# A two-layer convolution kernel on one Trainium2 core: an earlier sine table, an earlier second x load, and another order of ScalarE's and GpSimd's first steps

## What is computed

```python
def _implicit_filter(z, w1, b1, w2, b2, w3, b3, wo, freq, t, deltas):
    h = jnp.sin(freq * (z @ w1 + b1))
    h = jnp.sin(freq * (h @ w2 + b2))
    h = jnp.sin(freq * (h @ w3 + b3))
    h = h @ wo
    decay = jnp.exp(-t * jnp.abs(deltas))
    return h * decay
...
k = jnp.einsum('ijk,imk->ijmk', hx, hy)[0]
...
out = y + x * bias[:, None, None]
...
scores = jnp.einsum('bpsd,bptd->bpst', x, x) * inv_dim
red = jnp.sum(scores * weights[None], axis=-1, keepdims=True)
y = x + red
y_hat = (y - mean) * jax.lax.rsqrt(var + BN_EPS)   
return y_hat * gamma[None, :, None, None] + beta[None, :, None, None]
```

## Time and profile before

| | |
|---|---|
| median of three runs | 969.54 us |
| the profiled execution | 969.15 us |
| its span (first to last instruction) | 967.2 us |
| TensorE busy | 942.9 us, 97% |
| VectorE, ScalarE, GpSimd busy | 749.7, 684.9, 672.1 us |
| TensorE's mean granted clock | 0.993 of full speed |
| read and written in DRAM | 168.40 and 67.31 MB |

### The profile page before, as it was taken

How to read it: one execution, slowest core, us unless ns; L and a number is a source line. 1 busy time by engine, 2 the same in 40 slices (tenths; PEclk the granted TensorE clock), 3 DMA queues, 4 the chain that set the end, 5 groups by cost and what they waited for, 6 DMA issues and landing times.

```text
span 967.2 us, 18751 instructions
## 1 busy us (share of the span) xinstructions
PE 942.9 (97%) x5427; PEld 827.4 (86%) x5427; DVE 749.7 (78%) x2333; ACT 684.9 (71%) x1093; POOL 672.1 (69%) x519
## 2 busy tenths in 40 slices
PE   7999999999999999999999999999999999999993
PEld 5888888888888888888888888888888888888882
DVE  2677878878878878878878878778788788788785
ACT  3547777777777777777777777777777767767756
POOL 1767767767767767767777777777777777777750
PEclk9999999999999999999999999999999999999997
DMA  5865887878888877877788887776787887787634
GB/s 169 310 208 178 265 234 264 270 216 271 268 226 264 278 238 247 275 249 238 272 240 245 271 240 249 272 260 225 274 248 237 275 269 226 270 273 223 227 115 174
DMA packets 73310, 235.90 MB, mean 244 GB/s; under 512 B 7248, under 2 KB 24144, under 8 KB 65104
## 3 DMA queue, kind: packets, MB, share of 16 engines
q1 hardware_dynamic: 73296, 235.73, 75.7%
HBM read 168.40 MB, written 67.31 MB: 244 GB/s over the span
## 4 chain that ended last, share of the span: by engine, by line
PE 94%; ACT 2%; DVE 1%; DMA 1%; issue 0%; POOL 0%; SPq 0%; ACTq 0%; DVEq 0%
PE ps_c L518 36%; PE ps_u L518 31%; PE ps_z L518 27%; DMA xt_sb<-xt_in 1%; PE ps_avg L518 1%; ACT out_sb L493 1%; ACT z_sb L493 0%; DVE z_sb L715 0%; DMA par<-params_in 0%; POOL zl L414 0%; DVE products L737 0%; ACT zh L502 0%; DVE zl L726 0%; DMA filters_padded<-z_sb 0%; DVE stat L748 0%
## 5 line engine op out<-in xcount | busy, mean ns | idle before, releaser
L414 POOL TENSOR_TENSOR zl<-z_sb,zh 128x1024 fp32r<-128x1024 f32 x126 | 301.8, 2396 | 207.4 <-ACT zh L502 207.4
L737 DVE CUSTOM_DVE_ANT_0 products<-z_sb,ps_c 128x256 bf16<-128x256 f32 x508 | 183.7, 418 | 158.4 <-PE ps_c L518 158.4
L518 PE MATMUL ps_z<-uh,toep 128*128 128x512 f32 x768 | 270.7, 407 | 0.7 <-DVE ul L771 0.7
L472 ACT ACTIVATE uh<-ps_u 128x1024 fp32r<-128x1024 f32 x127 | 130.7, 1029 | 194.3 <-PE ps_u L518 194.3
L493 ACT ACTIVATE out_sb<-z_sb,shift,gain 128x256 f32<-128x256 f32 x496 | 257.7, 594 | 6.7
L518 PE MATMUL ps_u<-toep,xh 128*128 128x256 f32 x1016 | 239.8, 317 | 1.6 <-POOL toep L388 1.6
L518 PE MATMUL ps_c<-zh,wh 128*128 128x512 f32 x508 | 197.8, 389 | 1.5 <-DVE zl L726 0.7
L518 PE MATMUL ps_c<-zh,wl 128*128 128x512 f32 x508 | 198.1, 390 | 0.0
L518 PE MATMUL ps_c<-zl,wh 128*128 128x512 f32 x508 | 197.6, 389 | 0.0
L518 PE MATMUL ps_u<-toep_whole,xt_sb 128*128 128x128 f32 x1016 | 195.0, 273 | 0.0
L748 DVE BATCH_NORM_STATS2 stat<-z_sb 128x6 f32<-128x256 f32 x512 | 179.4, 414 | 0.0
(11 more groups left out here) (68 smaller groups left out, 925.8 us busy)
## 6 DMA issues: line engine op xcount, KB each, us to landing
xt_sb<-xt_in SPq DMA_DIRECT2D x64, 1024.0 KB, 9.3
x_sb<-x_in SPq DMA_DIRECT2D x128, 512.0 KB, 7.2
out<-out_sb SPq DMA_DIRECT2D x124, 512.0 KB, 3.5
w_sb<-wt_in SPq DMA_DIRECT2D x64, 256.0 KB, 6.8
toep_whole<-filters_padded SPq DMA_DIRECT2D x63, 256.0 KB, 6.7
out<-z_sb SPq DMA_DIRECT2D x4, 512.0 KB, 3.0
toep_whole<-filters_padded SPq DMA_DIRECT2D x2, 128.0 KB, 4.6
par<-params_in SPq DMA_DIRECT2D x1, 224.0 KB, 4.1
```

The costliest lines, as they stand in the source:

```text
L414: nc.gpsimd.tensor_tensor(zl[:, zs.slot(2)], z_sb[:, r, h], zh[:, zs.slot(2)].bitcast(F32), ALU.subtract)\
L472: nc.scalar.activation(uh[:, us.slot(2)], u_bank(us)[:, :, :, :], ACT.Copy)\
L518: return nc.tensor.matmul(o, a, b, start=start, stop=stop)
L737: last = nc.vector.tensor_tensor_reduce(products[:, cs.slot(2), k, b], z_sb[:, r, h, k, b], bank[:, k, b], 1.0 / math.sqrt(SIDE), 0.0, ALU ...
```

## The change

Five edits. ScalarE waits for the constants (four memsets of GpSimd) and takes a sine of one column (`sine_loaded`) before anything else. SyncE issues the x load of channel 1 right behind the weights of channel 0, ahead of the filter store and the Toeplitz loads. In the static steps up to 4 ScalarE's `round_u` (uh) stands at the head of the stage instead of behind the Toeplitz and weight roundings. GpSimd splits part 0 of channel 0's Toeplitz matrix (L392) behind xl(1) instead of ahead of it. TensorE waits for that part before y(0) (and y(1)) instead of before u(1).

```diff
--- before.py
+++ after.py
@@ -156,6 +156,7 @@
         par = sb("par", [P, NPARAM])
         freq_turns = sb("freq_turns", [P, 1])
         bias_turns = sb("bias_turns", [P, 3])
+        sine_loaded = sb("sine_loaded", [P, 1])
         ones = sb("ones", [P, P], F32R)
         minus_half = sb("minus_half", [P, 1])
 
@@ -297,6 +298,7 @@
 
             load_xt(0, 0)
             load_w(0, 0)
+            load_xt(1, 1)
 
             sp.wait_ge(filt_ready, 1)
             sp.dma_start(pad_dram[:, :, :].rearrange("f c n -> (f c) n"), filt[:, :])\
@@ -304,7 +306,6 @@
             sp.wait_ge(filt_stored, 16)
             load_first_toeplitz(1, first_s_landed)
             load_first_toeplitz(0, t_landed[0])
-            load_xt(1, 1)
 
             def stage(st):
 
@@ -378,20 +379,23 @@
                 if starts(ms):
                     shift_means(ms)
 
-                ts = st.trail(LAG_T)
-                if starts(ts):
+                def low_toeplitz(ts, parts):
+
                     t = ts.ring(2)
-                    parts = slice(0, 2)
-                    if first_channel(ts):
-                        parts = slice(0, 1)
-                        pool.wait_ge(first_sh_ready, 1)
-                        nc.gpsimd.tensor_tensor(toep[:, t, 1, 1], toep_whole[:, 0, 1],
-                                                toep[:, t, 1, 0].bitcast(F32), ALU.subtract)\
-                            .then_inc(first_sl_ready, 1)
                     wait_chan(pool, th_ready, ts, 1)
                     nc.gpsimd.tensor_tensor(toep[:, t, parts, 1], toep_whole[:, ts.ring(XR), parts],
                                             toep[:, t, parts, 0].bitcast(F32), ALU.subtract)\
                         .then_inc(tl_ready, 1)
+
+                ts = st.trail(LAG_T)
+                if starts(ts):
+                    if first_channel(ts):
+                        pool.wait_ge(first_sh_ready, 1)
+                        nc.gpsimd.tensor_tensor(toep[:, 0, 1, 1], toep_whole[:, 0, 1],
+                                                toep[:, 0, 1, 0].bitcast(F32), ALU.subtract)\
+                            .then_inc(first_sl_ready, 1)
+                    else:
+                        low_toeplitz(ts, slice(0, 2))
 
                 if active(st):
                     wait(pool, xh_ready, st, 1)
@@ -399,6 +403,9 @@
                     nc.gpsimd.tensor_tensor(xl[:, st.slot(4)], xt_sb[:, r, PAIR * h:PAIR * (h + 1), 0],
                                             xh[:, st.slot(4)].bitcast(F32), ALU.subtract)\
                         .then_inc(xl_ready, 1)
+
+                if starts(ts) and first_channel(ts):
+                    low_toeplitz(ts, slice(0, 1))
 
                 ws = st.trail(LAG_W)
                 if starts(ws):
@@ -422,6 +429,8 @@
         @block.scalar
         def _(act):
 
+            act.wait_ge(const_ready, 4)
+            nc.scalar.activation(sine_loaded[:, :], minus_half[:, :], ACT.Sin)
             for layer in range(3):
                 act.wait_ge(layer_done, 2 * layer + 2)
                 if layer == 0:
@@ -434,7 +443,19 @@
                     nc.scalar.activation(hid[:, half], part[:, half], ACT.Sin, scale=TWO_PI_BELOW)\
                         .then_inc(hid_ready, 1)
 
+            def round_u(us):
+
+                if active(us):
+                    wait(act, u_done, us, 1)
+                    wait(act, y_done, us, -1)
+                    nc.scalar.activation(uh[:, us.slot(2)], u_bank(us)[:, :, :, :], ACT.Copy)\
+                        .then_inc(uh_ready, 1)
+
             def stage(st):
+
+                filling = st.static() and st.number() <= 4
+                if filling:
+                    round_u(st.trail(LAG_U))
 
                 if active(st):
                     r, h = st.ring(XR), st.half()
@@ -465,12 +486,8 @@
                     wait(act, c_done, ws, -2)
                     nc.scalar.activation(wh[:, r], w_sb[:, r], ACT.Copy).then_inc(wh_ready, 1)
 
-                us = st.trail(LAG_U)
-                if active(us):
-                    wait(act, u_done, us, 1)
-                    wait(act, y_done, us, -1)
-                    nc.scalar.activation(uh[:, us.slot(2)], u_bank(us)[:, :, :, :], ACT.Copy)\
-                        .then_inc(uh_ready, 1)
+                if not filling:
+                    round_u(st.trail(LAG_U))
 
                 no = st.trail(LAG_NORM)
                 if starts(no) and not ending(no, 2):
@@ -542,6 +559,8 @@
 
             def product_y(zs):
 
+                if first_channel(zs):
+                    pe.wait_ge(tl_ready, 1)
                 wait(pe, ul_ready, zs, 1)
                 wait(pe, z_ready, zs, 0)
                 s, t = zs.slot(2), zs.ring(2)
@@ -578,9 +597,9 @@
                 us = st.trail(LAG_U)
                 if active(us):
                     r, t = us.ring(XR), us.ring(2)
-                    if first_channel(us) and not second_pair(us):
+                    if first_channel(us):
                         pe.wait_ge(first_sl_ready, 1)
-                    elif us.first_of_channel() or second_pair(us):
+                    elif us.first_of_channel():
                         wait_chan(pe, tl_ready, us, 1)
                     wait(pe, xl_ready, us, 1)
                     if not second_pair(us):
```

## The result

The changed kernel takes 966.01 us (median of 7 runs, 965.75 to 967.25) beside 969.41 us for the kernel before (7 runs, 969.20 to 969.57): ratio 0.9966, 95% interval 0.9955 to 0.9978. That is 3.4 us or 0.35% faster. The profiled execution took 965.97 us, with a span of 964.1.

The account below looks back on a forecast made before the run. TensorE, busy 97% of the span, bounds the kernel, so the gain is c(0)'s shift: store 1.05 (after 1.68 from the sine table) plus order 1.36, 2.41 us, giving 967.1 us on the median's scale; range 966.2 to 968.8.

Parts of the forecast that it names:

- Bound and marks: Opening: the gain is the shift of c(0), followed by store landing, u(0) and c(0); TensorE runs unbroken from c(0).
- Sine table: Opening, ScalarE: one table load left, beside the wait for `par`; first sine and store issue 1.68 us earlier.
- The store: Filter store's landing behind the early x load: at 14.0 instead of 15.05, 1.05 us earlier.
- its rival with 0.15: Filter store not held up by the early load: lands at 13.37, kernel at 966.5 us; chance 0.15.
- the laggard's time: Slowest DMA engine ahead of the store: ends at 10.5, needs 2.6 us more for the early load, 13.1.
- the free store: Store not delayed by the early x load: lands at 13.37, gain 3.04 us, 966.5 us; chance 0.15.
- The Toeplitz landing: First Toeplitz pair behind the store: u(0) kept at 5.07 us after the store's landing, no gain counted.
- The new order: First steps: u(1) directly behind u(0), uh(0) sooner, 1.2 us wait before u(2), c(0) 1.36 us earlier.
- The slower rival: Before u(0): store at 16.4, TensorE idle 4.6 us, clock halves, u(0) 1.2 us longer: 970.7 us; chance 0.05.
- The late Toeplitz load: Channel 1's Toeplitz load lands over 1.3 us late, u(2) waits, half of part 3 lost: 968.3 us; chance 0.06.
- part 3: Forecast term for the reordered first steps: c(0) at 32.88 instead of 34.24, 1.36 us.
- The end: Kernel's end: shifted end escapes the half clock, VectorE's 1.10 us wait goes, 966.0 us; chance 0.07.

Follow-up runs that it names:

- e14: Changed kernel with channel 1's x load back behind the first Toeplitz loads, second measurement: 966.32 us.
- e13: The changed kernel again, measured on one chip beside its variants: 966.02 us.
- e8: Changed kernel with channel 2's x load also issued early, behind channel 1's and ahead of the filter store: 967.96 us.
- e15: Changed kernel with ScalarE's old order in the first steps (uh behind the Toeplitz and weight roundings), repeat: 965.85 us beside 966.02.
- e16: Kernel before with the early sine and channel 1's early x load, none of the new order: 965.58 us beside 966.02 for the changed kernel.
- e1: Kernel before with the early sine alone: 967.60 us.
- e11: Changed kernel with ScalarE's old order and the 22 warming products cut into 13, a wait for the first Toeplitz part, and 3: 967.05 us.
- e4: Changed kernel with channel 1's x load back behind the first Toeplitz loads, first measurement, without the changed kernel beside it: 967.12 us.
- e9: Changed kernel with the 22 warming products cut into 13, a wait for the first Toeplitz part, and 3: 967.43 us.
- e12: Changed kernel with 10 warming products instead of 22 behind the filter: 967.69 us.

## Why the prediction went wrong, point by point

- **Bound and marks: right.** The gain is the shift of c(0), and no later wait appeared.
- **Sine table: right.** 1.68 forecast, 1.8 measured alone. In the changed kernel's trace the store is issued 1.84 us sooner, of which 0.2 come from `par`, landed at 3.1 instead of 3.3. Of the Trainium skill's two figures for a table load (ScalarE: Activation LUTs, What ACT_TABLE_LOAD costs) the 1.28 us is in the changed trace too, and nothing of a drain: the first activation starts at 2.03, 0.01 behind the load.
- **The store: the mis-sized term.** Forecast at 14.0, measured 13.37, the forecast's lower bound and its rival with 0.15. The step that failed is the laggard's time, the 0.6 us by which the early load was to hold up the store. I took 10.5 us for its end from one trace and added 2.6, which has the load landed near 13.5 (an estimate: 13.1 and some 0.35 for the end); in eleven of the twelve traces with it, it landed at 11.9 to 12.9, and the store's first bytes move 0.7 us behind its issue even with nothing ahead (e14: issue 11.29, bytes from 12.0 on). e14 against e13 gives 0.0 for the hold-up, the changed kernel's first trace 0.15. The mechanism was right, and only its size was off: where the load landed last, the store came 0.5 us behind it, the figure of the forecast. The Trainium skill's ring order (DMA: Bandwidth & Descriptors, HWDGE ordering) fits these traces and e8's 1.05 us. That the store landed at exactly the 13.37 of the free store is luck: it was issued 0.16 us sooner than forecast and took 0.16 longer than before.
- **The Toeplitz landing: a term left out.** I let the first pair land as before and looked only at what follows it. From the store's landing to u(0) it was 5.07 us and is 4.80, and part 0 comes 1.1 us sooner (4.74 behind the store instead of 5.88). e14 against e13 gives 0.4 us for the same. In the other traces with an early load part 0 comes 4.7 to 5.6 us behind the store, without it 5.9 to 6.1.
- **The new order: right in the trace, wrong in its credit.** c(0) is 12.91 us behind u(0), forecast 12.76, and the new wait before u(2) was forecast at 1.2 us and is 1.04. But I compared it with the old order *with x late*. With x early ScalarE's old order is the better one in the traces, by 0.4 us (e15) and 0.5 us with GpSimd's old order too (e16): part 0 has landed, nothing stands before uh(0), and the Toeplitz matrix of channel 1 is rounded in idle time. The rows for that were there: the prediction itself had uh(1) ahead of Toeplitz(1) cost TensorE 1.2 us, and did not ask what the old order would do once the load was moved.
- **The sum** of the profiled run: store 1.68 (forecast 1.05), landing 0.27 (0), fill 1.21 (1.36), together 3.16 against 2.41. On the medians the miss is 1.1 us, and 0.35 of it is neither: the profiled run of the kernel before lay 0.39 under its median, which the forecast added again, that of the changed kernel lies 0.04 under. So even with a free store (966.5 in the forecast) the time would have come out 0.5 too high: the landing's 0.27 and these 0.35, less 0.15 that the fill gave short.
- **The slower rival** had the right place and the wrong length: the clock fell there behind 1.79 and 2.13 us of idleness already (e1, e11), not only 4.6, though not in the changed kernel, whose store wasn't late. What I missed is the opposite case, warming products that run long.
- **The late Toeplitz load** did not occur. Its price was added up wrongly: 968.3 is 1.2 us above the forecast, nearly all of part 3 and not half of it.
- **The end: the rival's price was wrong.** That its 966.0 is the time measured is a coincidence: the end didn't change, and the last c ran at the low clock. VectorE's wait doesn't set the end. In the kernel before ScalarE's last rows ended at 962.6, last of all:

```profile
961.54 1.08 ACT L512 ACTIVATE z_sb<-z_sb,shift,gain 128x256 f32<-128x256 f32 x2
```

## What to carry to other kernels

When a change moves a load and reorders the work that waited for it, work out the old order with the load moved before giving the new one any credit: here the two early loads alone brought more (3.8 us) than the whole change (3.4). Here the store was delayed only by a load that still ran when the store's own bytes could leave, and moving that load out from between the critical Toeplitz loads and their landing gave time back there. And a variant has to stand beside its rival on one chip: 1.1 us of e4 shrank to 0.3 that way.

## What the runs showed of the hardware that I had not expected

TensorE's clock in the opening rises at a moment that differs from run to run of one program: 22 products of 512 columns took 5.3 us or 7.9. It fell again after an idle stretch of 1.79 us (e1) and of 2.13 us and three products (e11), and stayed up in the traces with 1.3 to 1.7 us and in e9 with 2.22. In e12 it rose within an idle stretch of 2.20 us. So the number of warming products has to hit between two costs, and in this kernel 22 did better than 10 or 13 and 3. The Trainium skill (TensorE: Matmul & The Clock Gate, Part 1: The HAM clock gate) says that the moment of the clock's rise varies between runs of the same kernel; these traces agree, by 2.6 us in the length of the warming.

A store of 192 KB behind loads of 1 MB in the same queue landed 1.87 us behind its issue, or 0.5 us behind the last of the loads, whichever was later (three traces with one load, one with two).
